# Attention before a mixture of experts: the projection of values from slot 11 to slot 5, the turning of gate rows from slot 12 to slot 6, the turning of values from slot 13 to slot 11

## The chip, the cores and the metric

One core of one Trainium2 chip runs the whole program in one launch. The metric is the device time of a run in microseconds (us). TensorE is PE in the profile (PEld is its weight load), VectorE is DVE, ScalarE is ACT, GpSimd is POOL, and SyncE's DMA queue is SPq.

## The reference

The input is 16 batches of 512 rows with 128 channels. Each batch first goes through an attention layer of 16 heads of 8 channels, then through a layer of 8 experts with a shared ninth one.

```python
x = x + layernorm(attention(layernorm(x)))
x = x + layernorm(experts(layernorm(x)))

# attention, for each batch of n = 512 rows
q, k, v = layernorm(x) @ w_qkv.T + b_qkv           # 16 heads x 8 channels
q, k = rope(elu(q) + 1), rope(elu(k) + 1)
attn = softmax(q @ k.T / sqrt(8))
out = attn @ v + depthwise_conv_of_3_taps(v)       # "lepe"
# experts: softmax gate, top 2 of 8, clipped swiglu of two products, plus a shared expert
```

## The kernel before, in words

The attention part is one schedule that is written out for each engine. `iteration(t)` runs for t from -3 to 15. In it, TensorE, ScalarE and VectorE step through 16 slots (`SLOTS`), and in each slot through four tiles (j = 0 to 3). Several batches are in work at once. In iteration t the softmax of batch t runs, the row maxima of batch t+1 are found, the queries and keys of batch t+2 are prepared, and the attention output of batch t-1 and the gate rows of batch t-2 are finished.

One slot holds, for each tile j:

- TensorE: `scores_t` (L757), the transposed scores of a head of batch t into one of two banks `psST`; it waits until ScalarE has read the tile two before. Then `scores` (L769), a score tile of batch t+1 into one of three banks `psS`; it waits until VectorE has read the tile three before. The two use different halves of the array's rows and run side by side.
- TensorE, once per slot after j = 1: `values` (L783), the four products of the previous slot's probabilities with V, which wait until all four exponentials of that slot are done. The page counts a float32 matmul twice, so a group is x8.
- TensorE, at the end of the slot: `misc(t, s)`, one small job that depends on the slot (a projection, a group of transposes, the gate's logits).
- ScalarE: four exponentials (L981) and then `extra(t, s)`, the copies of that slot, all in one queue.
- VectorE: four row maxima (L1117), and between them small steps that depend on slot and tile (`extra`, `gate`, `places`). The gate of a pair of batches runs in iterations 4, 6, 8, ..., 14 (`paired`), and fills slots 1 to 14 there with some twenty small steps. "Paired" below means these iterations.

The order around the change is set by hand. Before the change, the misc jobs are: slot 0 turning of x for batch t+2 (L794), 1 and 2 projection of queries and keys (L850), 3 turning of the maxima (L844), 4 turning of heads (L192), 5 to 7 nothing, 8 turning of lepe (L199), 9 turning of maxima (L844), 10 turning of heads (L192), 11 projection of values (L820), 12 turning of gate rows (L206), 13 turning of values (L827), 14 nothing, 15 logits and ranks (L213, L221, L223). ScalarE's copies are: slot 0 `copy_heads` (L892) and XT (L905), 1 and 2 the exponentials for the elu (L913), 4 the maxima (L964), 7 the first part of the queries (L921), 8 `copy_heads` and the first part of the keys (L892, L921), 9 and 10 the second parts (L925), 10 also the maxima (L964), 12 VT, the projected values (L934), 13 the middle tap of lepe (L941) and the turned gate rows (L235), 14 V, the turned values (L950, two instructions). After slot 8 the heads' copy must be done before the `values` group of slot 9 may start a new sum in `psPV`; slot 0 and slot 1 stand likewise.

All misc jobs share two banks of PSUM (`psM`). Which job has which bank follows from its place in the list `MISC`, by even and odd; `misc_freed` makes a job wait for the reader of the job before it in the same bank, by the table `READER`.

GpSimd has no slots. Its queue (`iteration(t)` at L1188) holds, in this order, the split of the maxima, the outer taps of lepe (which read VT), the floor of the elu exponentials, the second layernorm of batch t-2 (`normalise2`, L446, which makes the gate rows), scatters by indirect DMA, the rotation (L1212 to L1218), the split of the maxima of t+1, the residual parts (L1224, L1227) and the first layernorm of batch t+3. SyncE's queue stores and loads the parts of queries and keys, and stores the turned gate rows near its end of the iteration (`store_turned`, L246). In iteration 15 it goes on from there to load two of them back (L242) for the experts' first steps.

The copies that the change moves wait as follows: VT (L929 to L933) for the projection, for GpSimd's taps of the batch before and for the turning of the values before; V (L944 to L947) for its turning and for the products two batches before; the gate rows (L229 to L234) for their turning, for the logits and the store of two batches before.

Of the kernel before, what the change touches and what calls it, by code (L numbers as in the profile page):

```python
# [84 lines left out]
def due(count):  # L85

    return count > 0
# [381 lines left out]
def attention(nc, ends, x_in, wqkvT, chan, ones, rope_cos, rope_sin, ident, numbers, count, gate_wT, gate_b,  # L469
# [5 lines left out]
    with es:  # L475
# [93 lines left out]
        NCONST = 13  # L569
        LOADS = 2 * 16 * 2  # L570

        MISC = ["xT", "q", "k", "mT1", "O23", "lepeT", "mT0", "O01", "vT", "xT2", "V", "lg"]

        def misc_bank(use):
            return psM[MISC.index(use) % 2]
# [162 lines left out]
        @block.tensor  # L738
        def _(pe):
            pe.wait_ge(consts, 16 * NCONST)  # L740
            pe.wait_ge(lead, 2)

            def scores_t(t, h, kc, k):

                if kc == 0 and h % HALF == 0:
                    hf = h // HALF
                    pe.wait_ge(stacked[t.par][hf], t.done_par(LOADS))
                    pe.wait_ge(m_stacked[t.par][hf], t.done_par(32))
                banks = st_banks(t)
                if len(psST) <= k < len(banks):  # L750

                    pe.wait_ge(s_max, t.done(TILES, TILES))

                elif due(before := t.done(TILES, tile_before(psST if k < len(psST) else banks, k) + 1)):
                    pe.wait_ge(st_exp, before)
                rows = slice(SIDE * (h % 2), SIDE * (h % 2) + ROWS_ALL)
                nc.tensor.matmul(bank(st_banks(t), k)[:], KS[t.par][rows, h // 2, kc * P:(kc + 1) * P],  # L757
                                 QS[t.par][rows, h // 2, :], start=True, stop=True).then_inc(st_psum, 1)

            def scores(b, s, j, k):  # L760

                h, qc = max_tile(s, j)
                if j == 0 and s % HALF == 0:
                    pe.wait_ge(stacked[b.par][s // HALF], b.done_par(LOADS))

                if due(before := b.done(TILES, tile_before(psS, k) + 1)):
                    pe.wait_ge(s_max, before)
                rows = slice(SIDE * (h % 2), SIDE * (h % 2) + ROWS_QK)
                nc.tensor.matmul(bank(psS, k)[:], QS[b.par][rows, h // 2, qc * P:(qc + 1) * P],  # L769
                                 KS[b.par][rows, h // 2, :], start=True, stop=True).then_inc(s_psum, 1)  # L770

            def values(b, s):

                g, kc = divmod(s, QC)
                if s == 0:
                    pe.wait_ge(v_ready, b.done(1, 1))
                if kc == 0 and g % 2 == 0:

                    if due(before := b.done(2, g // 2)):
                        pe.wait_ge(ot_ready, before)  # L780
                pe.wait_ge(st_exp, b.done(64, 4 * s + 4))
                for j in range(HG):
                    last = nc.tensor.matmul(psPV[VW * j:VW * j + VW, :], V[b.par][:, kc, HG * g + j, :],  # L783
                                            PR[:, s % 2, j, :], start=(kc == 0 and g % 2 == 0), stop=(kc == QC - 1 and g % 2 == 1))
                last.then_inc(pv_done, 1)

            def misc(t, s):
                nxt, prep, prev = t + 1, t + 2, t + (-1)
                if s == 0 and prep.live:
                    misc_freed(pe, t, "xT")  # L790
                    pe.wait_ge(xn_ready, prep.done(1, 1))
                    m = misc_bank("xT")
                    for qc in range(QC):
                        last = nc.tensor.transpose(m[:, qc * P:(qc + 1) * P], XN[:, qc, :], IDF[:])  # L794
                    last.then_inc(xT_psum, 1)
                if s == 3 and t.live:
                    misc_freed(pe, t, "mT1")
                    max_transposes(t, 1, "mT1")
                if s == 1 and prep.live:
                    misc_freed(pe, t, "q")  # L800
                    project(prep, 0, "q")
                if s == 2 and prep.live:
                    misc_freed(pe, t, "k")
                    project(prep, 1, "k")
                if s == 4 and prev.live:
                    misc_freed(pe, t, "O23")
                    ends.turn_heads(pe, prev, 1, misc_bank("O23"))
                if s == 8 and prev.live:
                    misc_freed(pe, t, "lepeT")
                    ends.turn_lepe(pe, prev, misc_bank("lepeT"))  # L810
                if s == 9 and nxt.live:
                    misc_freed(pe, t, "mT0")
                    max_transposes(nxt, 0, "mT0")
                if s == 10 and t.live:
                    misc_freed(pe, t, "O01")
                    ends.turn_heads(pe, t, 0, misc_bank("O01"))
                if s == 11 and nxt.live:
                    misc_freed(pe, t, "vT")
                    pe.wait_ge(xT_ready, nxt.done(1, 1))
                    nc.tensor.matmul(misc_bank("vT")[:], WQKV[:, 2 * C:3 * C], XT[:, nxt.par, :],  # L820
                                     start=True, stop=True).then_inc(vT_psum, 1)
                if s == 13 and nxt.live:
                    misc_freed(pe, t, "V")
                    pe.wait_ge(vT_ready, nxt.done(1, 1))
                    m = misc_bank("V")
                    for kc in range(QC):
                        last = nc.tensor.transpose(m[:, kc * P:(kc + 1) * P], VT[:, 1 + kc * P:1 + (kc + 1) * P], IDF[:])  # L827
                    last.then_inc(v_psum, 1)
                old = t + (-2)
                if s == 12 and old.live:  # L830
                    misc_freed(pe, t, "xT2")
                    ends.turn_x(pe, old, misc_bank("xT2"))
                if s == 15 and (old.live or paired(t) is not None):
                    misc_freed(pe, t, "lg")
                if s == 15 and old.live and t.c < B - 1:
                    ends.logits(pe, old, misc_bank("lg"))
                if s == 15 and paired(t) is not None:
                    ends.ranks(pe, paired(t), misc_bank("lg"))

            def max_transposes(b, hf, use):  # L840
                pe.wait_ge(mx_step[hf], b.done(5, 5))
                m = misc_bank(use)[0:PARTS * HALF, 0:N // 2].bitcast(BF16)
                for qc in range(QC):
                    last = nc.tensor.transpose(m[:, qc * P:(qc + 1) * P],  # L844
                                               MP[:, hf, qc, :, :].rearrange("p a h -> p (a h)"), IDB[:])
                last.then_inc(mT_psum, 1)

            def project(b, w, use):
                pe.wait_ge(xT_ready, b.done(1, 1))
                nc.tensor.matmul(misc_bank(use)[:], WQKV[:, w * C:(w + 1) * C], XT[:, b.par, :],  # L850
                                 start=True, stop=True).then_inc(qk_psum[w], 1)

            def iteration(t):
                nxt, prev = t + 1, t + (-1)
                for s in range(SLOTS):
                    g, kc = divmod(s, QC)
                    for j in range(HG):
                        if t.live:
                            scores_t(t, HG * g + HEAD_AT[j], kc, 4 * s + j)
                        if nxt.live:  # L860
                            scores(nxt, s, j, 4 * s + j)

                        if j == (3 if t.c == B - 1 else 1):
                            if s == 0 and prev.live:
                                values(prev, SLOTS - 1)
                            if s > 0 and t.live:
                                values(t, s - 1)
                    misc(t, s)

            everywhere(iteration)(pe)  # L870
            values(Batch(B - 1), SLOTS - 1)
# [3 lines left out]
        def _(act):  # L875
# [18 lines left out]
            def extra(t, s):  # L894
# [30 lines left out]
                    nc.scalar.activation(PT[:, w, 1, :], RES[:, w, :], ACT.Copy).then_inc(part2[w], 1)  # L925
                if s == 10 and nxt.live:
                    copy_max(nxt, 0, "mT0")
                if s == 12 and nxt.live:
                    act.wait_ge(vT_psum, nxt.done(1, 1))  # L929
                    if due(before := nxt.done(2, 0)):  # L930
                        act.wait_ge(tap_added, before)
# [4 lines left out]
                if s == 13 and nxt.live:  # L936
                    act.wait_ge(vT_ready, nxt.done(1, 1))

                    if due(before := (nxt + (-2)).done(1, 1)):
                        act.wait_ge(lepeT_psum, before)  # L940
                    nc.scalar.activation(LP[:, nxt.par, :], VT[:, 1:N + 1], ACT.Identity,  # L941
                                         bias=CHAN[:, 6:7], scale=CHAN[:, 4:5]).then_inc(lepe_mid, 1)
                if s == 14 and nxt.live:
                    act.wait_ge(v_psum, nxt.done(1, 1))  # L944

                    if due(before := (nxt + (-1)).done(16, 0)):
# [4 lines left out]
                                                    source[:, :, g], ACT.Copy)  # L951
                    last.then_inc(v_ready, 1)
                old, p = t + (-2), paired(t)
                if s == 13 and old.live:
                    ends.copy_turned(act, old, misc_bank("xT2"))
                if s == 3 and p is not None:
                    ends.exponentials(act, p)
# [1176 lines left out]
```

## Time and profile before

| what | value |
| --- | --- |
| median of 3 runs | 1263.12 us (1261.43 to 1263.55) |
| time of the profiled execution | 1263.11 us |
| its span, from first to last instruction | 1261.2 us |
| busy: PE / DVE / ACT / POOL | 1063.0 / 1077.3 / 932.0 / 835.5 us |
| mean granted TensorE clock | 0.971 |
| costliest line | L1117 on DVE, 1024 row maxima of 680 ns, 696 us |
| next | L981 on ACT, 986 + 38 exponentials of 600 ns |

Attention fills the span up to about 886 us and the experts the rest. The chain of the page is followed back from the end and covers the experts' last stage alone, so what bounds attention has to be read from the timeline. Timeline rows give the start, the busy time, the engine, line and operation, and in brackets the idle time before it and who ended it. Rows of one line that follow each other are merged (x2, x4).

### The profile page before, as it was taken

To read this page: it belongs to the slowest core of one execution; us is meant where nothing else is said; L and a number is where in the kernel's file an instruction comes from. 1 tells how busy PE (TensorE), PEld (TensorE's weight loads), DVE (VectorE), ACT (ScalarE), POOL (GpSimd) and SP (SyncE) were. 2 spreads that over 40 slices of the span, in tenths; PEclk is the share of its full clock that TensorE was granted. 3 is DMA by queue.
4 is the path that set the end of the run, shared out by engine and by line. 5 is a ranking of instruction groups with operands and counts; after the bars stand their busy time and mean duration, and the time that the engine had idled before them with its cause. 6 is when DMAs were issued, how large, how long until landed. Compare 5 with 4: busy or idle time off the path is not lost. (4 is left out here: it accounts for less than half of the span.)

```text
span 1261.2 us, 21979 instructions
## 1 busy us (share of the span) xinstructions
PE 1063.0 (84%) x6376; PEld 445.6 (35%) x6376; DVE 1077.3 (85%) x2469; ACT 932.0 (74%) x1764; POOL 835.5 (66%) x1087
## 2 busy tenths in 40 slices
PE   1498999999999999999999999899899999887910
PEld 0012222222322222222222222222678778665600
DVE  2398899999999999999999999995587889999944
ACT  1117888888788778788888888879599888877712
POOL 5455466676578787888878878637264546776475
PEclk9999999999999999999999999999799999999965
DMA  2553432423424324234243242303134544454312
GB/s 67 116 126 121 105 85 59 116 71 86 97 84 113 93 89 124 78 102 103 78 107 95 82 119 69 88 19 111 51 101 145 192 150 156 129 157 136 114 50 79
DMA packets 108983, 128.21 MB, mean 102 GB/s; under 512 B 14224, under 2 KB 81844, under 8 KB 108596
## 3 DMA queue, kind: packets, MB, share of 16 engines
q1 hardware_dynamic: 98848, 105.94, 30.1%
q0 software_dynamic: 8192, 16.79, 4.8%
q10 hardware_dynamic: 1824, 4.06, 0.9%
q8 instruction: 53, 0.87, 0.3%
q14 instruction: 66, 0.54, 0.1%
HBM read 58.85 MB, written 59.51 MB: 94 GB/s over the span
## 5 line engine op out<-in xcount | busy, mean ns | idle before, releaser
L1117 DVE TENSOR_REDUCE MX<-psS 128x1 f32<-128x512 f32 x1024 | 647.5, 680 | 66.4 <-PE psS L769 64.6
L981 ACT ACTIVATE PR<-psST 128x512 f32<-128x512 f32 x986 | 535.9, 600 | 128.4 <-PE psST L757 126.4
L769 PE MATMUL psS<-KS,QS 48*128 48x512 bf16 x1024 | 372.1, 401 | 40.5 <-DMA KS<-scratch_parts 24.0
L757 PE MATMUL psST<-QS,KS 51*128 51x512 bf16 x986 | 338.8, 387 | 42.3 <-ACT PR L981 26.1
L783 PE MATMUL psPV<-PR,V 128*32 128x512 f32 x2048 | 275.6, 610 | 5.8 <-ACT PR L981 1.0
L757 PEld LDWEIGHTS psST<-QS,KS 51*128 51x128 bf16 x986 | 78.4, 93 | 400.2 <-ACT PR L981 368.5
L1987 POOL DMA_INDIRECT SHARED<-scratch_y,FROM x128 | 129.1, 1009 | 51.7 <-issue 37.9
L465 POOL DMA_INDIRECT scratch_x<-XN,POSI x128 | 130.5, 1020 | 36.3 <-issue 33.8
L769 PEld LDWEIGHTS psS<-KS,QS 48*128 48x128 bf16 x1024 | 87.2, 93 | 103.5 <-DVE MX L1117 71.6
L1572 PE MATMUL psY<-WD,HA 128*128 (+1 forms) x496 | 67.8, 279 | 13.6 <-issue 6.9
L1546 PE MATMUL psH<-XH,WS 128*128 128x512 f32 x169 | 74.1, 438 | 2.8 <-DVE XL L1743 1.9
L1572 PEld LDWEIGHTS psY<-WD,HA 128*128 128x128 f32 x496 | 63.3, 191 | 33.6 <-issue 31.7
L783 PEld LDWEIGHTS psPV<-PR,V 128*32 128x32 f32 x2048 | 40.8, 108 | 77.0 <-issue 63.0
L1646 ACT ACTIVATE A<-psH,DS 128x512 f32<-128x512 f32 x92 | 63.2, 687 | 5.4 <-PE psH L1548 1.8
L1548 PE MATMUL psH<-XH,WS 128*128 128x512 f32 x169 | 66.6, 394 | 0.0
L1547 PE MATMUL psH<-XL,WS 128*128 128x512 f32 x169 | 66.3, 392 | 0.0
L1227 POOL TENSOR_TENSOR PT<-RES,PT 128x512 bf16<-128x512 f32 x32 | 37.0, 1160 | 42.5 <-ACT PT L925 42.5
L1946 POOL TENSOR_SCALAR L<-L 128x512 f32<-128x512 f32 x30 | 18.7, 625 | 61.5 <-DVE L L1756 60.7
L1155 POOL TENSOR_SCALAR MP<-MX 128x32 bf16<-128x32 f32 x32 | 7.0, 217 | 72.0 <-DVE MX L1117 72.0
L446 POOL TENSOR_SCALAR XN<-X,MV,RS 128x128 f32<-128x128 f32 x64 | 51.9, 816 | 1.8
L406 POOL TENSOR_TENSOR RS<-VE,NHALF 128x4 f32<-128x4 f32 x48 | 49.7, 1035 | 4.0
L1234 POOL TENSOR_SCALAR XN<-X,MV,RS 128x128 f32<-128x128 f32 x64 | 50.1, 792 | 1.9
(217 smaller groups left out, 1851.0 us busy)
## 6 DMA issues: line engine op xcount, KB each, us to landing
scratch_parts<-PT SPq DMA_DIRECT2D x192, 128.0 KB, 2.4
QS<-scratch_parts SPq DMA_DIRECT2D x64, 192.0 KB, 3.4
KS<-scratch_parts SPq DMA_DIRECT2D x64, 192.0 KB, 4.4
XR<-scratch_x SPq DMA_DIRECT2D x46, 256.0 KB, 2.7
scratch_y<-YR SPq DMA_DIRECT2D x46, 256.0 KB
RES<-EL SPq DMA_DIRECT2D x64, 128.0 KB, 2.0
scratch_x<-ZERO SPq DMA_DIRECT2D x18, 256.0 KB, 2.2
X<-in_x SPq DMA_DIRECT2D x16, 256.0 KB, 5.0
```

The lines of the kernel that those rows point to most:

```text
L465: self.nc.gpsimd.indirect_dma_start(self.XG[int(b.c >= SPAN)][:, :], bass.IndirectOffsetOnAxis(ap=at, axis=0), self.XN2[:, b.c % 4, qc, :] ...
L757: nc.tensor.matmul(bank(st_banks(t), k)[:], KS[t.par][rows, h // 2, kc * P:(kc + 1) * P], QS[t.par][rows, h // 2, :], start=True, stop=Tru ...
L769: nc.tensor.matmul(bank(psS, k)[:], QS[b.par][rows, h // 2, qc * P:(qc + 1) * P], KS[b.par][rows, h // 2, :], start=True, stop=True).then_ ...
L783: last = nc.tensor.matmul(psPV[VW * j:VW * j + VW, :], V[b.par][:, kc, HG * g + j, :], PR[:, s % 2, j, :], start=(kc == 0 and g % 2 == 0), ...
L981: nc.scalar.activation(PR[:, s % 2, HEAD_AT[j], :], bank(st_banks(t), k)[:], ACT.Exp, scale=SCALE).then_inc(st_exp, 1)
L1117: nc.vector.tensor_reduce(out=MX[:, qc, h:h + 1], in_=bank(psS, k)[:], axis=AX.X, op=ALU.max).then_inc(s_max, 1)
L1546: nc.tensor.matmul(ps[:], matrix(p, 0, m, gl), XH[:, p % 2, :], start=True, stop=False)
L1547: nc.tensor.matmul(ps[:], matrix(p, 0, m, gl), XL[:, p % 2, :], start=False, stop=False)
L1548: nc.tensor.matmul(ps[:], matrix(p, 1, m, gl), XH[:, p % 2, :], start=False, stop=True).then_inc(h3_psum if m else h1_psum, 1)
L1572: last = nc.tensor.matmul(psY[:, q * P:(q + 1) * P], HA[:, p % HA_BUFS, q * P:(q + 1) * P], rows, start=routed(p), stop=routed(p) or q == ...
L1646: nc.scalar.activation(A1[:, p % 2, gl, :], hidden_bank(4 * p + 2 * gl)[:], ACT.Identity, bias=bias(p, 0, gl)).then_inc(a1_ready, 1)
L1987: nc.gpsimd.indirect_dma_start(GOT[:, b % G_BUFS, k, qc, :], None, YG[st][:, :], bass.IndirectOffsetOnAxis(ap=FROM[:, k, b * QC + qc:b * Q ...
```

## The change

Three TensorE jobs move to other slots of the iteration: the projection of values from 11 to 5, the turning of gate rows from 12 to 6, the turning of values from 13 to 11. ScalarE's copies of their results stay one slot behind: VT from 12 to 6, the gate rows from 13 to 7, V from 14 to 12. The middle tap of lepe (L941) stays in slot 13. The list that gives out the banks is put in the new order. No instruction is added or removed.

```diff
-        MISC = ["xT", "q", "k", "mT1", "O23", "lepeT", "mT0", "O01", "vT", "xT2", "V", "lg"]
+        MISC = ["xT", "q", "k", "mT1", "O23", "vT", "xT2", "lepeT", "mT0", "O01", "V", "lg"]
...
-                if s == 11 and nxt.live:
+                if s == 5 and nxt.live:
                     misc_freed(pe, t, "vT")
                     pe.wait_ge(xT_ready, nxt.done(1, 1))
                     nc.tensor.matmul(misc_bank("vT")[:], WQKV[:, 2 * C:3 * C], XT[:, nxt.par, :],
                                      start=True, stop=True).then_inc(vT_psum, 1)
-                if s == 13 and nxt.live:
+                if s == 11 and nxt.live:
                     misc_freed(pe, t, "V")
                     pe.wait_ge(vT_ready, nxt.done(1, 1))
...
-                if s == 12 and old.live:
+                if s == 6 and old.live:
                     misc_freed(pe, t, "xT2")
                     ends.turn_x(pe, old, misc_bank("xT2"))
...
-                if s == 12 and nxt.live:
+                if s == 6 and nxt.live:
                     act.wait_ge(vT_psum, nxt.done(1, 1))
...
-                if s == 14 and nxt.live:
+                if s == 12 and nxt.live:
                     act.wait_ge(v_psum, nxt.done(1, 1))
...
-                if s == 13 and old.live:
+                if s == 7 and old.live:
                     ends.copy_turned(act, old, misc_bank("xT2"))
```

## Rows read from the trace of the kernel before

**Rows 1.** Busy time by stretch (us, then PE, PEld, DVE, ACT, POOL): iterations 3 and 8.

```profile
246.00:295.00 49.00, 45.63 (x304) 13.23 (x302) 45.86 (x99) 41.43 (x81) 32.63 (x48) 1.00 0.34 89
498.00:550.00 52.00, 48.11 (x311) 14.31 (x311) 50.56 (x120) 41.63 (x81) 41.75 (x59) 1.00 0.35 92
```

**Rows 2.** Timeline of iteration 5, slots 7 and 8, with no misc job.

```profile
366.26 1.07 PE L783 MATMUL psPV<-PR,V 128*32 128x512 f32 x8
...
367.69 1.09 ACT L981 ACTIVATE PR<-psST 128x512 f32<-128x512 f32 x2 [0.79 <-PE psST L757]
...
369.14 1.07 PE L783 MATMUL psPV<-PR,V 128*32 128x512 f32 x8
```

**Rows 3.** Timeline of iteration 5, slots 11 and 12.

```profile
377.96 1.07 PE L783 MATMUL psPV<-PR,V 128*32 128x512 f32 x8
...
378.47 2.13 ACT L981 ACTIVATE PR<-psST 128x512 f32<-128x512 f32 x4
...
379.89 1.12 PE L820 MATMUL psM<-XT,WQKV 128*128 128x512 f32 x2
...
381.49 1.07 PE L783 MATMUL psPV<-PR,V 128*32 128x512 f32 x8
```

**Rows 4.** Timeline of iteration 5, slots 13 to 15.

```profile
385.92 0.66 PE L827 MATMUL psM<-IDF,VT 128*128 128x128 f32 x4
...
387.25 1.07 PE L783 MATMUL psPV<-PR,V 128*32 128x512 f32 x8
387.46 0.60 ACT L235 ACTIVATE SHARED<-psM 128x512 f32<-128x512 f32 x1
387.94 2.17 ACT L981 ACTIVATE PR<-psST 128x512 f32<-128x512 f32 x4
...
390.49 1.07 PE L783 MATMUL psPV<-PR,V 128*32 128x512 f32 x8
```

**Rows 5.** Timeline of iteration 1, slots 14 and 15, where batch -1 has no gate rows.

```profile
188.01 1.07 PE L783 MATMUL psPV<-PR,V 128*32 128x512 f32 x8
...
190.89 1.06 PE L783 MATMUL psPV<-PR,V 128*32 128x512 f32 x8
```

**Rows 6.** Timeline of iteration 5, slots 2 and 3, with the projection of keys.

```profile
352.03 0.39 PE L757 MATMUL psST<-QS,KS 51*128 51x512 bf16 x1
...
353.94 1.07 PE L783 MATMUL psPV<-PR,V 128*32 128x512 f32 x8
```

**Rows 7.** Timeline of iteration 5, slots 5 and 6.

```profile
361.65 0.38 PE L757 MATMUL psST<-QS,KS 51*128 51x512 bf16 x1
...
363.31 1.06 PE L783 MATMUL psPV<-PR,V 128*32 128x512 f32 x8
```

**Rows 8.** Timeline of iteration 5, slots 7 and 8: ScalarE.

```profile
368.65 0.63 ACT L921 ACTIVATE PT<-ROT 128x512 bf16<-128x512 f32 x1
...
370.57 1.08 ACT L981 ACTIVATE PR<-psST 128x512 f32<-128x512 f32 x2 [0.31 <-PE psST L757]
```

**Rows 9.** Timeline of iteration 8 (paired), slots 11 to 14: a score tile, and VectorE's idle time.

```profile
535.07 0.39 PE L769 MATMUL psS<-KS,QS 48*128 48x512 bf16 x1
...
542.97 1.29 DVE L1117 TENSOR_REDUCE MX<-psS 128x1 f32<-128x512 f32 x2 [0.49 <-PE psS L769]
```

**Rows 10.** Timeline: ScalarE in iteration -1, GpSimd in iteration 15, the experts' first step.

```profile
76.46 0.63 ACT L925 ACTIVATE PT<-RES 128x512 bf16<-128x512 f32 x1 [6.49 <-POOL RES L1224]
...
857.56 4.43 POOL L446 TENSOR_SCALAR XN<-X,MV,RS 128x128 f32<-128x128 f32 x4
...
862.17 1.06 PE L783 MATMUL psPV<-PR,V 128*32 128x512 f32 x8
...
886.47 1.15 ACT L1637 ACTIVATE XH<-ROT 128x512 fp32r<-128x512 f32 x2 [0.65 <-PEq L475]
```

**Rows 11.** Iteration 10, slot 10: the timeline, and busy time by stretch (clock seventh).

```profile
630.39 1.75 PE L783 MATMUL psPV<-PR,V 128*32 128x512 f32 x8
...
631.00:632.00 1.00, 1.00 (x8) 0.00 (x0) 1.00 (x3) 0.00 (x0) 0.00 (x0) 0.50 0.61 171
```

## The prediction

> **What bounds the kernel now.** I read the busy time by stretch first. In iteration 3, unpaired, TensorE is busy for 45.63 us of 49.00, VectorE for 45.86 and ScalarE for 41.43; in iteration 8, paired, VectorE has 50.56 of 52.00 [rows 1]. No engine is full in the first, so a loop of waits sets its pace; in the second VectorE does. Then I read the timeline of iteration 5, slot by slot. The mark I measure by is the start of the `values` group, one per slot (L783). I call the time from one to the next the step of a slot; it holds that slot's misc job and the copies that ScalarE does after the slot before it, so the projection in slot 11 and the copies of slot 10 share a step.
>
> The plain step, in slot 7, where there is no misc job and no copy ahead, is 369.14 - 366.26 = 2.88 us [rows 2]. The loop can be read there: from the `values` group to the start of the third exponential 1.43 us (the group itself, then the transposed scores that the exponential reads), two exponentials 1.09, and 0.36 from their end (368.78) to the next group, which must have them. ScalarE idles for 0.79 us in it [rows 2], so one copy a slot fits free, and two copies don't. On TensorE a turning of 0.66 us fits too: the one of slot 13 starts at 385.92 and ends 0.67 us before the group of 387.25 [rows 4], and of this the loop leaves only 0.36 to TensorE. Any step above 2.88 has a cause of its own, and the change touches four such places.
>
> **The change, part by part**, unpaired iterations first.
>
> Slot 11 loses the projection and gets the turning of V. Its step is 381.49 - 377.96 = 3.53 us [rows 3]. Two copies of slot 10 hold the exponentials up until 378.47, so tile 3 comes late, and the projection starts at 379.89 and then stands alone for 1.12 us. With the turning (0.66 us [rows 4]) TensorE is free at 380.55. The four exponentials end at 378.47 + 2.13 = 380.60, and the group follows 0.36 later [rows 2], at 380.96. The step is 3.00: **-0.53 us**. What is late next is ScalarE.
>
> Slot 14 loses the copy of the gate rows, which came behind the middle tap of lepe. Its step is 390.49 - 387.25 = 3.24 [rows 4]. Iteration 1 shows the same slot without that copy, with the tap there: 190.89 - 188.01 = 2.88 [rows 5]. **-0.36 us**.
>
> Slot 5 gets the projection. A like job is the projection of keys: from tile 3's transposed scores to the next group 353.94 - 352.03 = 1.91 us [rows 6]. In slot 5 tile 3 starts at 361.65, so the group moves from 363.31 to 363.56 [rows 7]: +0.25. The step after it is 366.26 - 363.31 = 2.95 [rows 7, 2], 0.07 over plain, because VectorE still works off its debt of slots 2 to 5 there; with 0.25 more time this goes. Together **+0.18 us**.
>
> Slot 8 gets the gate rows' copy, behind the first part of the queries (L921), and before the heads' copy that the group of slot 9 waits for. The copy holds the queue for 387.94 - 387.46 = 0.48 us [rows 4], 0.12 less than its busy time; by the same discount L921 holds it for 0.51. From 368.65 on, two copies and two exponentials (1.08) end at 370.72, where the third exponential now starts at 370.57 [rows 8]: **+0.15 us**.
>
> At nothing I cost: the turning of gate rows in slot 6 (as in slot 13, covered by the loop's wait for exponentials; without that cover 0.66); VT's copy of slot 6 and V's of slot 12 (0.69 and some 0.7 us, alone in their slots, covered by the 0.79 of idle time; each lands in a slot that had none or had VT); slots 12 and 13, where nothing heavier comes, and slot 15, where V's copies go and the logits stay, so I leave the step as it is (a gain of 0 to 0.2 us is possible). Nothing moves on VectorE or GpSimd. The queues that the moved steps pass: behind VT's wait on ScalarE stand the first parts of the queries and keys, for which GpSimd waits. VT needs the projection one slot earlier, done by then, and GpSimd's taps, which stand second in its queue. Only in iteration -1, where ScalarE has no exponentials and just waits, does VT come ahead of them in earnest; there the second parts wait for GpSimd for 6.49 us anyway [rows 10], so 0, at most 2 us.
>
> The turning of gate rows now needs GpSimd's `normalise2` by slot 6. The tightest place is iteration 15: it ends there at 857.56 + 4.43 = 861.99, and the group of slot 6 starts at 862.17, with the misc job behind it [rows 10]. It holds. Iteration 15 runs by ScalarE's queue alone, so the copy costs the same in slot 7 as in 13: 0. SyncE's store of those rows is freed earlier there, but the experts' first step is released by the end of TensorE's attention block [rows 10], not by a load: 0.
>
> **Paired iterations.** From slot 5 to 13 VectorE is the bound. In iteration 8 TensorE still waits for it in slot 12: the second score tile of slot 12 starts only at 535.07, just ahead of the group [rows 9], when VectorE has freed its bank, so taking the projection from slot 11 gives nothing. VectorE's first idle time comes only at 542.97 [rows 9]. For the same reason the projection in slot 5 and the copy in slot 7 should be taken in. The gate copy's 0.36 in slot 14 lies behind that stretch and stays: **-0.36**.
>
> Sum: seven unpaired iterations with gate rows (2, 3, 5, 7, 9, 11, 13) at 0.18 + 0.15 - 0.53 - 0.36 = -0.56 make -3.9; iterations 0 and 1, without gate rows, at 0.18 - 0.53 = -0.35 make -0.7; six paired ones at -0.36 make -2.2. That is -6.8 us against the profiled execution's 1263.11 us (span 1261.2), which is the median of the runs, 1263.12, to within 0.01. Forecast: **1256.3 us**.
>
> **A rule against it.** Where TensorE waits, the granted clock can fall to half. In iteration 10, after waits for VectorE in slots 7 to 10, it was 0.50, the 1.2 GHz level, and the `values` group took 1.75 us instead of 1.07 [rows 11]. The Trainium skill, "TensorE: Matmul & The Clock Gate" (Part 1), says that the throttled state is the default and that activity releases it. By that rule a schedule that leaves slots 12 to 14 without misc jobs could lose the clock there. The trace speaks against it: slots 5 to 7 were three empty slots in a row, and iteration 3 kept 1.00 over its whole length [rows 1].
>
> **The rivals.**
>
> A. *The half clock comes in slots 12 to 14* (slower). The price is at least 1.75 - 1.07 = 0.68 us each time [rows 11]. In the fifteen iterations 0 to 14 that would be +10.2, and 1256.3 + 10.2 = 1266.5 us. It cancels the gain from ten times on and makes the kernel slower by 0.2% from fourteen on. Against it: rows 1, as above. Chance 0.05, of which some lies between.
>
> B. *VectorE becomes the bound where the projection left.* It is busy for 45.86 of 49.00 us even unpaired [rows 1], and its own steps crowd slots 9 to 12. If it holds slot 12 at its old time, nine times 0.53 are lost: 1261.1 us, within 0.2%. By half, 1258.7. For it: only 3.1 us of idle time in the iteration. Against it: the change takes 0.56 of that. Chance 0.12.
>
> C. *Paired iterations don't take in the new load*: TensorE's score tiles come late enough in slots 6 and 7 to let VectorE idle. Six times 0.25 + 0.15 is +2.4: 1258.7 us. For it: nothing reads directly. Against it: VectorE's unbroken work [rows 9]. Chance 0.13.
>
> D. *Nothing is gained*, since what leaves slots 11 and 14 comes back whole at slots 5 and 7: +1.12 a time there instead of 0.25, and 0.48 instead of 0.15. Fifteen times 0.87 and fourteen times 0.33 (the sites less the iterations where there are none) would give +17.7, so 1274 us. It would need steps with no slack on either engine, against the 0.79 of idle time [rows 2]. Chance 0.03.
>
> E. *More gain*: half-clock stretches like that of iteration 10 move or vanish, or slot 15 gains its 0.2: 1254. Chance 0.07.
>
> **How the numbers follow.** The forecast has 0.60. The range of 1253.5 to 1260.5 us takes in E, C and half of B, and leaves out A, D and the whole of B, some 0.13 together. A measurement of this kernel tells 0.2%, or 2.5 us, from no change, so faster means below 1260.6: forecast, C, E and half of B, with something off for sums that miss, 0.85. Within 0.2%: the other half of B and the milder part of A, 0.10. Slower: D and the rest of A, 0.05.
>
> **What would show it.** In iteration 5 of the changed kernel the step of slot 11 should be near 3.0, that of slot 14 2.88, slot 5 3.13, slot 6 2.88, slot 8 3.2; iteration 3 should be shorter by about 0.5 and iteration 8 by 0.4. The experts' part should keep its length. If slot 11 stays at 3.5 with TensorE waiting for VectorE, B is right; a granted clock of 0.5 in slots 12 to 14 is A; a first `values` wait for GpSimd's gate rows in slot 6 would be a cause that I have excluded.

## The result and the profile after

The changed kernel is slower. Thirteen runs have a median of 1265.29 us (1264.05 to 1269.29), against 1262.43 us (1261.3 to 1264.66) for thirteen runs of the kernel before on the same chip: a ratio of 1.0026, 95% interval 1.0019 to 1.0034. The forecast was 1256.3 us, its range 1253.5 to 1260.5.

The profiled execution took 1264.05 us, its span was 1262.2 us: 1.0 us more than before. From the page of the changed kernel, the engines' busy time, the clock line in 40 slices and three groups (line, engine, operation; busy us, mean ns of one; idle time before, and who ended most of it):

```profile
PE 1054.3 (84%) x6376; PEld 446.8 (35%) x6376; DVE 1076.2 (85%) x2469; ACT 931.7 (74%) x1764; POOL 836.0 (66%) x1087
...
PEclk9558999999999999999999999999899999999965
...
L1117 DVE TENSOR_REDUCE MX<-psS 128x1 f32<-128x512 f32 x1024 | 647.1, 678 | 67.6 <-PE psS L769 64.1
L981 ACT ACTIVATE PR<-psST 128x512 f32<-128x512 f32 x986 | 536.0, 600 | 132.3 <-PE psST L757 127.8
L769 PE MATMUL psS<-KS,QS 48*128 48x512 bf16 x1024 | 368.0, 401 | 46.4 <-DMA KS<-scratch_parts 29.1
```

The busy times of VectorE, ScalarE and GpSimd moved by at most 1.1 us; TensorE's fell by 8.7. What speaks of a loss is the last row: idle time of TensorE ahead of the scores, ended by the load of the keys, is 29.1 us, and in the page before it was 24.0. The difference of 5.1 us is in the main one wait of 5.51 us, and it lies before iteration 0. I cut the span at the first `values` groups (L783) of iterations 0 and 15 and at the last one (98.29, 852.19 and 883.23 us before, 102.84, 852.31 and 884.08 after):

| piece of the span, us | before | after | difference | forecast |
| --- | --- | --- | --- | --- |
| up to the first `values` group of iteration 0 | 98.29 | 102.84 | +4.55 | 0 |
| iterations 0 to 14 | 753.90 | 749.47 | -4.43 | -6.8 |
| iteration 15 | 31.04 | 31.77 | +0.73 | 0 |
| from the last `values` group to the end | 377.97 | 378.12 | +0.15 | 0 |

So two thirds of the expected gain are there, and a loss ahead of the loop cancels them.

**The start.** In iteration -1 TensorE has only score tiles to do, ScalarE a few copies, and SyncE loads the parts of queries and keys that iteration 0 needs. The end of iteration -1 in the kernel before (timeline of ScalarE, SyncE's last loads and the first `values` group; ACTq is ScalarE's DMA queue):

```profile
83.85 0.69 ACT L934 ACTIVATE VT<-psM,CHAN 128x512 f32<-128x512 f32 x1 [5.18 <-PE psM L820]
...
87.26 0.93 SPq L719 DMA_DIRECT2D KS<-scratch_parts  x2
...
89.22 0.38 ACT L950 ACTIVATE V<-psM 128x256 f32<-128x256 f32 x1 [3.83 <-PE psM L827]
...
90.64 0.36 ACTq L2065 DMA_DIRECT2D W<-in_w1T  x1
91.03 0.45 ACTq L2065 DMA_DIRECT2D W<-in_w3T  x1
91.51 0.45 ACTq L2065 DMA_DIRECT2D WD<-in_wdT  x1
...
98.29 1.94 PE L783 MATMUL psPV<-PR,V 128*32 128x512 f32 x8
```

The three rows of ACTq are the experts' weights (1152, 1152 and 594 KB), which ScalarE asks for at the head of its iteration 0, behind all of iteration -1. Nobody needs them until the experts. In the changed kernel, all its engines' timeline:

```profile
68.31 0.69 ACT L934 ACTIVATE VT<-psM,CHAN 128x512 f32<-128x512 f32 x1 [9.45 <-PE psM L820]
...
83.30 0.38 ACT L950 ACTIVATE V<-psM 128x256 f32<-128x256 f32 x1 [4.22 <-PE psM L827]
...
84.76 0.37 ACTq L2065 DMA_DIRECT2D W<-in_w1T  x1
84.87 0.84 SPq L719 DMA_DIRECT2D QS<-scratch_parts  x2
85.16 0.45 ACTq L2065 DMA_DIRECT2D W<-in_w3T  x1
85.64 0.45 ACTq L2065 DMA_DIRECT2D WD<-in_wdT  x1
87.95 4.67 SPq L719 DMA_DIRECT2D KS<-scratch_parts  x2
92.76 0.63 PE L757 MATMUL psST<-QS,KS 51*128 51x512 bf16 x1
98.90 0.61 PE L769 MATMUL psS<-KS,QS 48*128 48x512 bf16 x1 [5.51 <-DMA KS<-scratch_parts]
102.84 1.94 PE L783 MATMUL psPV<-PR,V 128*32 128x512 f32 x8
```

V's copy waited for its turning in slot 13; the turning is now in slot 11, and the copy starts 5.9 us earlier (83.30 against 89.22). ScalarE has nothing left to wait for, so 2898 KB of weights are asked for from 84.76 on, just ahead of the first of SyncE's eight loads of queries and keys (84.87 to 87.95), where they had come behind all eight. The last pair of those needs 4.67 us only to be issued, where it had needed 0.93, and TensorE then stands for 5.51 us. The issues between 75 and 104 us, before and after (KB each, median us from issue to landing; ahead of them what each queue moved: packets, MB, share of the 16 engines; q1 is SyncE's, q10 ScalarE's):

```profile
q1 hardware_dynamic: 3122, 2.67, 43.0%
q10 hardware_dynamic: 504, 2.99, 25.8%
...
QS<-scratch_parts SPq DMA_DIRECT2D x4, 192.0 KB, 4.2
KS<-scratch_parts SPq DMA_DIRECT2D x4, 192.0 KB, 5.1
```

```profile
QS<-scratch_parts SPq DMA_DIRECT2D x4, 192.0 KB, 13.3
KS<-scratch_parts SPq DMA_DIRECT2D x4, 192.0 KB, 14.0
```

A load of 192 KB that landed after 5 us lands after 14. The Trainium skill, "DMA: Bandwidth & Descriptors" (Queues, rings and completion order), says that each DMA engine serves its queues in turn, one packet at a time. The rows fit that: a packet of q10 is 2.99 MB / 504 = 5.9 KB, one of q1 2.67 MB / 3122 = 0.86 KB, so a turn each would give the weights several times the bytes. No run varied the size of the packets, and none shows that a packet of these rows is what is served in one turn, so that part is not shown.

**The loop.** In iteration 5 (timeline, slots 11 to 14; rows 3 and 4 of before answer to it):

```profile
381.09 1.07 PE L783 MATMUL psPV<-PR,V 128*32 128x512 f32 x8
381.54 2.13 ACT L981 ACTIVATE PR<-psST 128x512 f32<-128x512 f32 x4
...
382.97 0.66 PE L827 MATMUL psM<-IDF,VT 128*128 128x128 f32 x4
383.21 1.28 DVE L1117 TENSOR_REDUCE MX<-psS 128x1 f32<-128x512 f32 x2
...
383.95 0.39 PE L769 MATMUL psS<-KS,QS 48*128 48x512 bf16 x1
...
384.27 1.07 PE L783 MATMUL psPV<-PR,V 128*32 128x512 f32 x8
...
390.03 1.06 PE L783 MATMUL psPV<-PR,V 128*32 128x512 f32 x8
...
392.91 1.07 PE L783 MATMUL psPV<-PR,V 128*32 128x512 f32 x8
```

Slot 14 has the step 392.91 - 390.03 = 2.88, as forecast. Slot 11 has 384.27 - 381.09 = 3.18, not 3.00. The exponentials end at 381.54 + 2.13 = 383.67, and 0.36 later would be 384.03. What comes late is the score tile of 383.95, which waits for VectorE to free its bank (383.21 + 0.64 = 383.85). Summed by place, the steps of iterations 0 to 14 give:

| term | sites | forecast each | measured each | forecast, us | measured, us |
| --- | --- | --- | --- | --- | --- |
| slots 5 and 6, unpaired | 9 | +0.18 | +0.19 | +1.6 | +1.67 |
| slot 8, unpaired | 7 | +0.15 | +0.18 | +1.1 | +1.29 |
| slot 11, unpaired | 9 | -0.53 | -0.36 | -4.8 | -3.25 |
| slot 14 | 13 | -0.36 | -0.355 | -4.7 | -4.61 |
| slots 4 to 7, paired (all in iteration 14) | 6 | 0 | +0.04 | 0 | +0.25 |
| slots 8 to 13, paired | 6 | 0 | -0.09 | 0 | -0.54 |
| slot 2 of iterations 9, 11, 13 | 3 | 0 | +0.28 | 0 | +0.84 |
| slot 10, unpaired | 7 | 0 | +0.04 | 0 | +0.29 |
| slot 1, unpaired (nearly all in iteration 0) | 9 | 0 | | 0 | -0.36 |

These sum to -4.42. The -0.36 of slot 1 belongs to the start: that step lies where the clock comes back to full, and it differs from -0.87 to +0.20 over the profiles of the experiments. The -0.54 is made of half-clock stretches: two in the kernel before (iterations 10 and 12), one in the changed one (iteration 6).

**Iteration 15** (timeline): the gate rows come from GpSimd, and their turning now stands in slot 6.

```profile
857.68 6.19 POOL L446 TENSOR_SCALAR XN<-X,MV,RS 128x128 f32<-128x128 f32 x4
...
862.30 1.06 PE L783 MATMUL psPV<-PR,V 128*32 128x512 f32 x8
...
864.02 0.63 PE L206 MATMUL psM<-IDF,XN 128*128 128x128 f32 x4 [0.66 <-POOL XN L446]
865.12 1.07 PE L783 MATMUL psPV<-PR,V 128*32 128x512 f32 x8
```

TensorE waits for GpSimd (0.66 us); the step is 2.82 where it was 1.94.

### The profile page after: what moved, and what is told of

Its sections match the earlier page's. It is cut to its first block and busy times, and to the rows that moved or that the text cites. A ratio compares the mean times of both kernels' runs of the same rounds, so it can differ in the third digit from the quotient of the medians.

```text
span 1262.2 us, 21979 instructions
## 1 busy us (share of the span) xinstructions
PE 1054.3 (84%) x6376; PEld 446.8 (35%) x6376; DVE 1076.2 (85%) x2469; ACT 931.7 (74%) x1764; POOL 836.0 (66%) x1087
## 5 line engine op out<-in xcount | busy, mean ns | idle before, releaser
L769 PE MATMUL psS<-KS,QS 48*128 48x512 bf16 x1024 | 368.0, 401 | 46.4 <-DMA KS<-scratch_parts 29.1
L783 PE MATMUL psPV<-PR,V 128*32 128x512 f32 x2048 | 274.1, 607 | 5.9 <-ACT SHARED L892 1.2
L1572 PE MATMUL psY<-WD,HA 128*128 (+1 forms) x496 | 67.7, 279 | 13.4 <-DVE HA L1772 6.8
L783 PEld LDWEIGHTS psPV<-PR,V 128*32 128x32 f32 x2048 | 40.8, 108 | 77.9 <-issue 64.6
L446 POOL TENSOR_SCALAR XN<-X,MV,RS 128x128 f32<-128x128 f32 x64 | 53.7, 844 | 1.8
```

The lines of the kernel that those rows point to most:

```text
L1572: last = nc.tensor.matmul(psY[:, q * P:(q + 1) * P], HA[:, p % HA_BUFS, q * P:(q + 1) * P], rows, start=routed(p), stop=routed(p) or q == ...
```

## The experiments

**How to read them.** The first eight kernels ran on another chip. There the kernel before took 1329.55 us (the first four) and 1328.98 us (the next four), and by the profiles the experts' part was 58 to 64 us longer. The attention part ran slower there as well: with the order of the kernel before (experiment 4) iterations 0 to 14 took 1.6 us more than in the rows above and iteration 15 took 5.1 us more. The intervals are about 0.25% wide to each side, so for these the verdict rests on the trace: the start of the first `values` group, and the steps of undisturbed unpaired iterations, compared with the profile of before. That profile comes from the other chip; experiments 2 and 4 show what the old order does on this one. The last four ran on a chip where the kernel before took 1262.42 us (19 runs), which decides their times.

**1. The changed kernel, its weights asked for later.**

```diff
 # SyncE, end of its iteration
+                if t.c == -1:
+                    sp.wait_ge(ones_set, 1)
+                    load_weights(sp)
 # ScalarE, head of its iteration 0
-                    act.wait_ge(ones_set, 1)
-                    load_weights(act)
```

> The changed kernel, with one thing undone: the experts' weights are loaded by SyncE's queue at the end of iteration -1, behind the loads of batch 1's queries and keys, as they were by time in the kernel before, and no longer by ScalarE. Theory W (ScalarE, done with V two slots earlier, issues 3 MB of weights before SyncE's last loads of batch 1, and these land late): the first values group comes at about 98 us again instead of 102.84, no wait for keys is left at slot 0 of iteration 0, and the time is about 5 us under the changed kernel's, 1260 us or a ratio of 0.998 to the kernel before. Rival P (the parts of batch 1 are stored late because their copies stand behind VT on ScalarE): the stall stays, 1265 us. Rival C (the half clock up to 105 us): it stays too, 1265 us.

Measured: 1328.61 us, ratio 0.9986 (0.9962 to 1.001). The first `values` group starts at 97.70 us. Its DMA issues between 75 and 104 us:

```profile
QS<-scratch_parts SPq DMA_DIRECT2D x4, 192.0 KB, 5.0
KS<-scratch_parts SPq DMA_DIRECT2D x4, 192.0 KB, 5.9
```

Behind SyncE's own loads, the weights disturb nothing, and the whole +4.55 us is gone (97.70 against 102.84, and 0.6 less than before). The three jobs stand as in the change and the first group still starts at half clock (1.74 us; 1.07 later on), so neither parts stored late nor the clock makes the wait.

**2. The kernel before, its weights asked for earlier.**

```diff
+                if s == 12 and t.c == -1:
+                    act.wait_ge(ones_set, 1)
+                    load_weights(act)
```

The call at the head of ScalarE's iteration 0 goes.

> The kernel before, with one thing of the change: ScalarE issues the weights in slot 12 of iteration -1, right behind VT, at about 84.6 us instead of 89.2. Everything else stands as before. Theory W: keys of batch 1 land late, the first values group comes 3 to 5 us later (102 us), and the time is 1265 to 1267 us, slower than before by 0.2 to 0.4%. Rivals P and C: no change, 1262.4 us.

Measured: 1336.28 us, ratio 1.0056 (1.0031 to 1.0081). TensorE's wait and the first `values` group (timeline):

```profile
98.34 0.60 PE L769 MATMUL psS<-KS,QS 48*128 48x512 bf16 x1 [4.54 <-DMA KS<-scratch_parts]
...
102.28 1.93 PE L783 MATMUL psPV<-PR,V 128*32 128x512 f32 x8
```

The loads land after 13.2 and 14.0 us. None of the change's three jobs has moved here, and the wait is there: when the weights are asked for makes it. The last pair of loads took only 1.83 us to issue here, so the long issue is not what makes the wait.

**3. The changed kernel, the gate rows of iteration 15 at their old place.**

```diff
-                if s == 6 and old.live:
+                if s == (12 if t.c == B - 1 else 6) and old.live:
...
-                if s == 7 and old.live:
+                if s == (13 if t.c == B - 1 else 7) and old.live:
```

> The changed kernel, but in iteration 15 the gate rows are turned in slot 12 and copied in slot 13, as before the change. Theory: in iteration 15 the turning in slot 6 waits for GpSimd's normalise2, which took 6.19 us there, and that costs 0.7 to 0.9 us; then this kernel takes 0.8 us less than the changed one, and the step of slot 6 is 1.95 instead of 2.82. Rival: the wait hides later in the iteration, or the rows' copy in slot 8 costs more there than in slot 14: 0.3 us or less.

Measured: 1332.67 us, ratio 1.0033 (1.0005 to 1.0061); first group 104.05. In iteration 15, against the changed kernel's profile, slot 6 takes 0.89 us less, slot 8 0.49 less and slot 14 0.49 more. The copy costs the same 0.49 wherever it stands. The 0.89 is not the edit's alone, since GpSimd's gate rows took less time here (timeline):

```profile
864.50 4.40 POOL L446 TENSOR_SCALAR XN<-X,MV,RS 128x128 f32<-128x128 f32 x4
```

Where they take 4.4 us, slot 6 is only 0.18 to 0.19 longer than before even with the rows left early (experiments 1, 5 and 12). The forecast of 0.8 us for the edit is not borne out by the time either (1332.28 us for the changed kernel on this chip).

**4. The kernel before with the edit of experiment 1**, a control.

> The kernel before, with the weights loaded by SyncE's queue at the end of iteration -1. By time that is within 1 us of where ScalarE issued them. Theory W: no change, 1262.4 us within 0.1%, first values group at 98.3. If it is faster or slower by over 1 us, moving the issue from one queue to the other has an effect of its own, and the run on the changed kernel must be corrected by it.

Measured: 1331.1 us, ratio 1.0013 (0.9986 to 1.004); first group 97.87, against 98.29 in the profile of before, on the other chip. The time shows no effect of the queue; the 0.4 us at the start lie between profiles of two chips, so no effect of the place is shown either.

**5. The changed kernel again**, on this chip.

> The changed kernel once more, on the chip of the three runs that are sent with it. Expected: 1.0026 of the kernel before, as measured (0.2% slower), and the first values group at 102 to 104 us.

Measured: 1332.28 us, ratio 1.0046 (1.0015 to 1.0078); first group 104.47, loads landing after 13.1 and 13.4 us. In iteration 15, slot 6 is only 0.19 us longer than before, with no wait for GpSimd.

**6. Only the values' half of the change.** The kernel before, with the projection in slot 5 (copy 6) and the turning in 11 (copy 12); the gate rows stay.

```diff
-        MISC = ["xT", "q", "k", "mT1", "O23", "lepeT", "mT0", "O01", "vT", "xT2", "V", "lg"]
+        MISC = ["xT", "q", "k", "mT1", "O23", "vT", "lepeT", "mT0", "O01", "V", "xT2", "lg"]
```

> The kernel before with only the projection and the turning of values moved (slots 5 and 11, copies in 6 and 12); the gate rows stay in 12 and 13, in the other bank. The weights stay with ScalarE, which comes to them early. Theory W: all of the lost start is in this part, so the first values group comes at about 102 us. Of the steady iterations it brings slot 5 +0.25, slot 6 -0.08, slot 11 -0.35 in the unpaired ones, and slot 14 keeps 3.23. Together about -1 from iterations 0 to 14 and +4.6 from the start: 3.5 us slower than the kernel before, ratio 1.003. Iteration 15 unchanged. Rival (the loss is in the gate rows' move): no slower than before.

Measured: 1334.37 us, ratio 1.0051 (1.0024 to 1.0077); first group 102.72. Slot 5 is 0.25 longer in iterations 0 to 14, slot 11 shorter by 0.37 to 0.46 in the unpaired ones (0.42 to 0.44 in most), slot 14 there as before. Slot 11 in iteration 5 (timeline):

```profile
381.23 1.06 PE L783 MATMUL psPV<-PR,V 128*32 128x512 f32 x8
381.73 2.13 ACT L981 ACTIVATE PR<-psST 128x512 f32<-128x512 f32 x4
...
383.27 1.28 DVE L1117 TENSOR_REDUCE MX<-psS 128x1 f32<-128x512 f32 x2
...
384.00 0.39 PE L769 MATMUL psS<-KS,QS 48*128 48x512 bf16 x1
...
384.32 1.07 PE L783 MATMUL psPV<-PR,V 128*32 128x512 f32 x8
```

ScalarE alone would put the group at 381.73 + 2.13 + 0.36 = 384.22; it starts 0.10 later, again behind a score tile that waited for VectorE. In the changed kernel that lag was 0.24. The values' half brings the whole loss at the start.

**7. Only the gate rows' half.** The kernel before, with their turning in slot 6 and their copy in slot 7.

> The kernel before with only the gate rows moved (turned in slot 6, copied in slot 7), values in 11 and 13 as before. Theory: no loss at the start (first values group at 98.3), slot 14 from 3.23 to 2.88 in thirteen iterations (-4.6), slot 8 +0.17 in seven (+1.2), iteration 15 +0.7 by the wait for GpSimd: -2.7 us, ratio 0.998. Rival (the loss at the start comes with any of the moved copies): first group at 102, ratio 1.001.

Measured: 1330.3 us, ratio 1.0007 (0.9985 to 1.0029); first group 98.02. Slot 14 is 0.35 shorter in unpaired iterations, slot 8 0.17 and slot 10 0.04 longer, slot 11 0.05 shorter. No loss at the start: the two halves are told apart. Two things fell short of what was expected. The wait for GpSimd in iteration 15 did not come (slot 6 is 0.19 longer, not 0.7). And slot 14 of iterations 6, 8, 10 and 12 is 0.35 to 1.04 us longer than in the profile of before, not 0.36 shorter; with the old order on this chip it is 0.31 to 0.41 longer (experiment 2). The time is not below that of the kernel before, and the ratio of 0.998 that was expected lies just outside the interval.

**8. The values' half, weights as in experiment 1, and the gate rows in slots 13 and 14**, into the place that V leaves.

```diff
 # TensorE
-                if s == 12 and old.live:
+                if s == 13 and old.live:
 # ScalarE
-                if s == 13 and old.live:
+                if s == 14 and old.live:
```

> A version that should beat both: values in slots 5 and 11 with copies in 6 and 12, as changed; the gate rows one slot later than before instead of six earlier (turned in 13, copied in 14, a slot whose copy has left); the weights issued by SyncE's queue behind batch 1's loads. Theory: the start is kept (first group at 98), slot 14 falls to 2.88 without slot 8 rising, iteration 15 has no wait. Slot 15 may rise by 0 to 0.2 where copy and logits meet. Sum: slots 5 and 6 +1.9, slot 11 -3.2, slot 14 -4.6: about -5.5 us against the kernel before, ratio 0.9955. Rival (logits in slot 15 wait for the copy of slot 14): slot 15 +0.3 in thirteen iterations, -1.5 us, ratio 0.999.

Measured: 1326.16 us, ratio 0.998 (0.9956 to 1.0005); first group 97.78. In unpaired iterations slot 14 is 0.35 shorter and slots 8 and 15 are as before. ScalarE's second copy has gone from slot 13, as in the change, but costs nothing where it lands. The expected ratio was 0.9955; experiment 11 repeats the kernel on the other chip.

**9. The changed kernel with one weight early**: the first 1152 KB from ScalarE as in the change, the rest from SyncE as in experiment 1.

> The changed kernel, with one of the three large weight loads (W1, 1.15 MB of 2.90 MB) left where ScalarE issues it early, and the rest by SyncE's queue behind batch 1's loads. If the loads of batch 1 are late because they share the DMA engines with the bytes in front, the loss at the start is about the share of those bytes: first values group at 99.5 to 101 us. If it is the issuing of any transfer by ScalarE at that place that hurts, it is 102 us or more; if W1 is small enough to hide, 98.

Measured: 1259.37 us, ratio 0.9973 (0.9962 to 0.9984); first group 97.77. Its DMA issues between 75 and 104 us:

```profile
QS<-scratch_parts SPq DMA_DIRECT2D x4, 192.0 KB, 6.1
KS<-scratch_parts SPq DMA_DIRECT2D x4, 192.0 KB, 6.7
```

With 1152 KB in front the loads land hardly later than in the profiles with none in front (4.2 to 5.8 and 5.1 to 6.9 us), and the start is not late at all. So the price does not grow evenly with the KB in front: with 1152 KB nothing is lost, with 2898 KB 4.0 to 6.2 us (first group at 102.28 to 104.47). Where between the two it begins was not tried.

**10. The changed kernel with both mends** (experiments 1 and 3).

> The changed kernel with both repairs: weights behind batch 1's loads, and in iteration 15 the gate rows in slots 12 and 13. Expected: first values group at 98, iterations 0 to 14 at -4.4 against the kernel before as in the changed kernel, iteration 15 at 0: -4.5 to -5 us, ratio 0.9963. Rival (more is lost elsewhere, in the experts' part): 0.999 to 1.001.

Measured: 1257.69 us (1256.3 to 1258.8), ratio 0.9965 (0.9952 to 0.9978). In its profile the first group starts at 97.22, iterations 0 to 14 take 4.0 us less than before, and iteration 15 takes the same (L446 took 4.44 us). The span is 1254.5 us, 6.7 less than before; 1.6 of that lie behind the last `values` group.

**11. The kernel of experiment 8** on this chip.

> The version with the gate rows in slots 13 and 14, once more, for its ratio on this chip. From the steps of its slots: 5 to 6 us under the kernel before, ratio 0.996; on the first try 0.998 with an interval of 0.9956 to 1.0005.

Measured: 1256.25 us (1254.87 to 1257.53), ratio 0.9955 (0.9942 to 0.9968): 6.2 us below the kernel before, and the lowest median of all (its interval and that of experiment 10 overlap). First group 97.39; iterations 0 to 14 take 7.0 us less, slot 11 -0.43 in most unpaired iterations, slot 14 -0.36, slot 8 nothing. In iteration 15 the copy moves 0.5 us from slot 14 to slot 15, and the iteration takes the same. The span is 1253.0 us.

**12. The changed kernel a third time.**

> The changed kernel beside the two repaired ones. Expected: 1.0026 of the kernel before, and 0.6% over the repaired ones.

Measured: 1265.08 us, ratio 1.0022 (1.001 to 1.0034); first group 103.98, iterations 0 to 14 -4.95, iteration 15 +0.03. GpSimd's gate rows in iteration 15 (timeline):

```profile
858.30 4.44 POOL L446 TENSOR_SCALAR XN<-X,MV,RS 128x128 f32<-128x128 f32 x4
```

So the changed kernel is slower on both chips, and each of its profiles has the late start. The wait for GpSimd in iteration 15 comes and goes: it was there in the first profile and in experiment 9 (6.19 us for L446, slot 6 longer by 0.88), but not here or in experiments 1 and 5. Why the same four instructions take 4.4 or 6.2 us stays open.

## Why the prediction was wrong

Slower had a chance of 0.05, and the two mechanisms given it were not the one that came.

**The step that failed: iteration -1.** The prediction said that only there VT comes ahead of the queries' and keys' parts in earnest, "so 0, at most 2 us". It looked at what stands behind the moved VT, and was right about that: the second parts start at 76.86 against 76.46 [rows 10]. It did not follow the other moved copy, V, to the end of ScalarE's iteration -1, where the next thing in the queue is a DMA. That a step which comes earlier starts transfers earlier, and that these meet others, was not in the sum. It cost 4.55 us in the profile (5.7 in the third one). Experiments 1 and 2 show the cause from both sides, experiments 6 and 7 the half of the change that brings it, the values' one. SyncE's own queue was named, but only for iteration 15.

**Slot 11, -0.53 each.** A term that was mis-sized: -0.36, and -0.43 without the gate rows' copy in slot 8. ScalarE was taken as the next thing late; it was VectorE, by 0.24 us in iteration 5. That is rival B (chance 0.12), for a third of its price. Why the copy in slot 8 adds to VectorE's lateness three slots later wasn't tried. I take it that VectorE waits in the longer slot 8 and cannot make that up, but this is argued, not shown.

**Slots 5, 6, 8 and 14** came within 0.03 us a place, and in unpaired iterations experiments 6 and 7 give the same steps one half at a time. Five of the six paired iterations took in the load of slots 5 and 7 to within 0.01 us; iteration 14 did not and paid the whole 0.25 of slot 5, here and in experiments 6 and 11. So rival C holds for one iteration of six, at 0.25 us instead of 2.4. The -0.36 in slot 14 was bought at 0.18 in slot 8, though: experiments 8 and 11 have it for nothing, because one slot on from the old place there is room. The prediction costed the change without asking whether it was the cheapest place.

**Iteration 15, "It holds".** It rested on one duration of L446 (4.43 us) against a mark 0.18 us later, which was too thin a margin for a program whose profiles give 4.4 or 6.2 for the same four instructions. It holds in two of the changed kernel's profiles and fails in the first. The price was 0.7 us. Otherwise slot 6 is 0.2 longer and slots 12 and 13 are as much shorter, 0.03 in all.

**Rival A** did not make the result: three slots without misc jobs (12 to 14) kept the full clock, 2.4 GHz, in every iteration of the profile. The steps of slot 14 are 2.88 in unpaired iterations, and no `values` group there is at the half rate. But it is not out altogether. In experiment 3's profile the granted clock was 0.50, the 1.2 GHz level, over slots 13 to 15 of iteration 13 (busy time by stretch, as in rows 11):

```profile
796.70:807.00 10.30, 9.79 (x42) 1.55 (x38) 6.86 (x12) 6.11 (x13) 3.53 (x8) 0.50 0.33 79
```

TensorE had idled 0.97 us for VectorE just before, at 795.74. The three steps are 0.72, 1.31 and 1.35 us longer than in the changed kernel's profile, 3.4 us together. Of the seven profiles with slots 12 to 14 free of misc jobs it is the only one that shows this. The two with the old order on that chip (experiments 2 and 4) have no half clock in slots 12 to 15 of iterations 0 to 14, but experiments 7 and 8, with a job in slot 13, have a stretch there as well (slots 14 and 15 of iteration 10, slots 12 and 13 of iteration 4). Whether the empty slots favour it is not shown. The rule of the Trainium skill in "TensorE: Matmul & The Clock Gate" (Part 1) did not decide the result. **Rival D** is out: slot 5 costs 0.25 a time, not 1.12. **Rival E** came in part, by one half-clock stretch less (-0.54); slot 15 gained nothing.

**The sum.** -6.8 forecast, +0.85 measured at the last `values` group. The difference of 7.7 us is 4.55 (start), 2.4 (loop: 1.5 in slot 11, 0.8 in slot 2, the rest small) and 0.7 (iteration 15). The medians are 2.9 us apart where the two profiled executions are 0.9 us apart. The third profile (experiment 12, an execution of 1265.08 us) is 2.0 us above that of before: start +5.7, iterations 0 to 14 -4.95, iteration 15 nothing, and +1.3 behind the last `values` group, where the order is the same. So part of the 2.9 is the spread of single executions.

## What to carry to other kernels

When a step moves earlier in an in-order queue, follow that queue to its next DMA, in the iterations at the edges too: large loads that nobody is waiting for can jump ahead of small ones that somebody is. Such loads belong behind the urgent ones; in the same queue they stay there whatever moves (experiments 1 and 4). And a job is cheapest in a slot whose bound is another engine: moving the gate rows by one slot into the place just left gave the same gain as moving them by six, at no price in the loop.

## What the runs showed of the hardware that was not expected

- **Large loads of one queue against small ones of another.** Landing of 192 KB loads (queries, keys): 4.2 and 5.1 us with the weights behind them, 6.1 and 6.7 with 1152 KB in front, 13.3 and 14.0 with 2898 KB. The queue that issues is held too: the last two loads took 4.67 us to issue instead of 0.93, and from 1.83 to 4.80 in the six profiles with 2898 KB in front.
- **VectorE and GpSimd hold each other up.** In iteration 11 the step of slot 2 is 0.40 us longer than before, though nothing was moved there. Before (timeline, one row of each engine):

```profile
655.43 1.45 POOL L1181 TENSOR_TENSOR SHARED<-SHARED,TAP 128x512 f32<-128x512 f32 x1
655.47 0.28 DVE L386 TENSOR_TENSOR SHARED<-OH,CAND 128x128 f32<-128x128 bf16 x1
```

After:

```profile
656.13 1.27 POOL L1181 TENSOR_TENSOR SHARED<-SHARED,TAP 128x512 f32<-128x512 f32 x1
656.27 1.28 DVE L386 TENSOR_TENSOR SHARED<-OH,CAND 128x128 f32<-128x128 bf16 x1
```

  Before, VectorE ran through in 0.28 us and GpSimd took 1.45; after, GpSimd had its 1.27 and VectorE took 1.28, ending 0.15 us behind it (657.55 against 657.40). In iterations 9 and 13 VectorE also ends 0.14 to 0.15 us behind GpSimd, before and after, and how long it takes (0.91 and 1.16 us before, 1.25 and 1.26 after) goes by how early it came. The Trainium skill, "SBUF — State Buffer" (SBUF: two separate sides), says that, for a VectorE operation with two SBUF inputs against a GpSimd operation that reads SBUF, whichever of the two starts first holds the shared port pair for its whole instruction and the other waits. The rows after agree: VectorE starts 0.14 us behind and ends behind GpSimd. In the rows before, GpSimd's starts 0.04 us earlier and yet VectorE runs through, so the order in which they took the ports cannot be read there. A shift of 0.1 us between two engines went with 1.0 us on VectorE. VectorE's extra time in iterations 9, 11 and 13 (0.34, 1.00 and 0.10 us) goes with the +0.35, +0.40 and +0.10 of slot 2, which are its +0.84. Like the wait of iteration 15 it comes and goes: in experiment 5 VectorE came 0.9 to 1.0 us after GpSimd, took 0.39 to 0.49, and slot 2 is not longer.
- **The granted clock's record has gaps.** The mean clock was 0.971 before and 0.942 after, and the clock line has "55" where before it had "99". Yet the float32 turning of V in iteration -1 took 1.12 us in both (0.66 later on), and the first `values` group 1.94 us in both: both kernels ran their start at 1.2 GHz, and only one record says so. There the durations are to be believed.
